# A graph network kernel: node rows split into a rounded part and a remainder, spread by float32r products

## The reference

```python
edge_index = jnp.stack([src, dst])
x = _layernorm(x + _L0_gnn_ref(...))   # relu projection, 2 x (messages of 8 edge types, sum by dst, GRU), out
x = _layernorm(x + _L1_gnn_ref(...))   # 3 x (relation matrices, mean per relation, sum by dst, root, relu)
x = _layernorm(x + _L2_gnn_ref(...))   # GCN: norm[:, None] * x[col], sum by row, W
x = _layernorm(x + _L3_gnn_ref(...))   # mean of edge attributes by row and by col, 2-layer MLP
...
            trans = jnp.einsum('nh,tdh->tnd', h, edge_W[l])
            msgs = trans[edge_type, src]
            agg = jax.ops.segment_sum(msgs, dst, num_segments=num_nodes)
            h = _gru_cell(agg, h, gru_wih[l], gru_whh[l], gru_bih[l], gru_bhh[l])
```

## Time and profile before

| what | value |
|---|---|
| median of 3 runs | 2964.3 us (2952.74 to 2971.47) |
| span of the profiled execution | 2969.2 us |
| PE matmul busy | 2492.2 us, 84% |
| PE weight loads busy | 2211.7 us, 74% |
| DVE busy | 1808.3 us, 61% |
| POOL busy | 1585.9 us, 53% |
| ACT busy | 868.5 us, 29% |
| HBM traffic | 174 GB/s over the span |

### The profile page before, as it was taken

One profiled execution on the slowest core, in us unless ns is written; L12 is line 12 of the kernel. 1 busy time (PEld: TensorE's weight loads), 2 busy tenths in 40 slices (PEclk: granted clock), 3 DMA queues, 4 the chain that ended last, 5 costly groups with the idle time before them and its releaser, 6 DMA issues.

```text
span 2969.2 us, 45704 instructions
## 1 busy us (share of the span) xinstructions
PE 2492.2 (84%) x15625; PEld 2211.7 (74%) x15625; DVE 1808.3 (61%) x6126; ACT 868.5 (29%) x1546; POOL 1585.9 (53%) x1706
## 2 busy tenths in 40 slices
PE   7587878888687899746999998998989897878798
PEld 3366666666387889436999997888988886777797
DVE  4565656575576777423876655676865554433585
ACT  2355555554354111213222231111311110443102
POOL 0656666663577666542566626666456665565200
PEclk9789888888799999857999999999999999898899
DMA  7312112110398666106888887877788774565793
GB/s 273 111 50 53 51 51 53 51 52 25 103 281 260 166 173 170 38 27 210 274 272 270 269 266 231 240 228 211 238 273 251 226 234 134 174 213 198 232 267 105
DMA packets 271515, 520.11 MB, mean 175 GB/s; under 512 B 61999, under 2 KB 115554, under 8 KB 270501
## 3 DMA queue, kind: packets, MB, share of 16 engines
q1 hardware_dynamic: 185053, 289.49, 31.2%
q0 software_dynamic: 86224, 227.59, 26.6%
HBM read 323.93 MB, written 192.99 MB: 174 GB/s over the span
## 4 chain that ended last, share of the span: by engine, by line
PE 69%; issue 10%; DMA 7%; DVE 6%; another core or an unknown queue 4%; ACT 2%; POOL 2%; SPq 0%; DVEq 0%; POOLq 0%; ACTq 0%
PE ps L1058 21%; PE ps L1030 10%; PE ps L892 7%; PE ps L1043 6%; PE ps L1245 5%; PE ps L1289 4%; PE ps L886 4%; PE ps L878 4%; DMA chunks<-xs 2%; DMA rec<-chunks,idx 2%; DMA srow<-lanes_of_slots 1%; DVE shot L2033 1%; POOL attributes L744 1%; PE ps L1112 1%
## 5 line engine op out<-in xcount | busy, mean ns | idle before, releaser
L735 POOL DMA_INDIRECT rec<-chunks,idx x596 | 588.5, 987 | 500.5 <-PE ps L1058 184.9
L1058 PE MATMUL ps<-dhot,rec 128*128 128x168 f32 x4768 | 757.2, 312 | 70.4 <-issue 35.3
L1058 PEld LDWEIGHTS ps<-dhot,rec 128*128 128x128 f32 x4768 | 703.8, 194 | 99.6 <-issue 77.6
L2054 DVE TENSOR_SCALAR dhot<-iota,dcode 128x168 f32<-128x168 f32 x2384 | 584.6, 311 | 216.7 <-remote 102.4
L1030 PE MATMUL ps<-hrow,shot 126*128 126x128 f32 x4000 | 516.3, 284 | 63.8 <-issue 29.5
L735 POOL DMA_INDIRECT msg<-messages,idx_buf x416 | 398.2, 957 | 307.3 <-issue 189.7
L1030 PEld LDWEIGHTS ps<-hrow,shot 126*128 126x128 f32 x4000 | 493.7, 199 | 81.7 <-issue 65.9
L1386 ACT ACTIVATE xs<-ps 128x512 f32<-128x512 f32 x500 | 295.1, 597 | 763.5 <-PE ps L1030 393.8
L744 POOL DMA_INDIRECT attributes<-w,rank_to x352 | 353.2, 1004 | 213.1 <-issue 102.2
L2033 DVE TENSOR_SCALAR shot<-srow,lane_no 126x512 f32<-126x512 uint8 x500 | 230.2, 486 | 117.4 <-PE ps L1030 51.2
L892 PE MATMUL ps<-big,lane1h 128*128 128x300 f32 x832 | 231.6, 432 | 9.3 <-issue 8.0
(11 more groups left out here) (304 smaller groups left out, 2538.6 us busy)
## 6 DMA issues: line engine op xcount, KB each, us to landing
chunks<-xs SPq DMA_DIRECT2D x375, 256.0 KB
tmp<-inverse_counts SPq DMA_DIRECT2D x36, 1008.0 KB
chunks<-xs SPq DMA_DIRECT2D x125, 258.0 KB
srow<-lanes_of_slots SPq DMA_DIRECT2D x100, 320.0 KB
grec<-chunks SPq DMA_DIRECT2D x125, 256.0 KB
messages<-big SPq DMA_DIRECT2D x25, 504.0 KB
trow<-lanes_of_targets SPq DMA_DIRECT2D x30, 320.0 KB
rec<-chunks,idx POOLq DMA_INDIRECT x596
```

Of the source, the lines that this page charges most:

```text
L735: eng.indirect_dma_start(buf, None, table, bass.IndirectOffsetOnAxis(ap=index, axis=0)).then_inc(sem, 16)
L1058: last = mm(ps[:, 4 + i % 2, (v % 3) * WT:(v % 3 + 1) * WT], rec[:, v % RS, j * P:(j + 1) * P], dhot[:, v % DS, j * WT:(j + 1) * WT], star ...
L2054: last = vec.tensor_scalar(dhot[:, v % DS, j * WT:(j + 1) * WT], iota[:, 0:WT], dcode[:, v, j:j + 1], None, ALU.is_equal)
```

## The change

`shot`, `thot`, `hrow` and `yrows` become float32r. ACT's copy from PSUM so leaves a rounded row in `hrow`. DVE then subtracts it from what is still in PSUM and keeps the remainder, also float32r (`keep_lows`, for the GCN `keep_target_lows` into `ylows`). In `spread_slots` and `spread_target` each float32 product becomes two float32r products into the same PSUM columns, one with the rounded rows and one with the remainders. PE's waits for `rows_kept` and `gcn_rows` become waits for `lows_kept`.

The remainders need room. For layer 1 they lie over `x`, which SP loads again from its input after layer 1's tiles; for layers 2 to 4 they lie over `nodes`, which SP stores to HBM in layer 1 and loads back after layer 4's tiles. The lists `code`, `idx`, `dcode` and `deg_part` move to the buffers of the layers, and several semaphores are merged into `window_step` and `degree`. The path for graphs that don't fit the slots (`general`, not taken here) adds both parts of `yrows` again.

```diff
+F32R = mybir.dt.float32r
...
+        nodes_d = nc.dram_tensor("node_counts", (P, NP), F32).ap()
...
-        x = sb("x", [P, NV])
+        with nc.sbuf_tensor("x", [P, NV], F32) as x:
+            pass
+        low_1 = sb("low_1", [P, TB, P], F32R)
         h = sb("h", [P, NV])
         res = sb("res", [P, NV])
         acc = sb("acc", [P, NP])
-        nodes = sb("nodes", [P, NP])
+        with nc.sbuf_tensor("nodes", [P, NP], F32) as nodes:
+            pass
+        low_2 = sb("low_2", [P, NB, P], F32R)
         tmp = sb("tmp", [P, 8, 512])
...
-                hrow = two("hrow", [P, TB, P])
...
+                hrow = two("hrow", [P, TB, P], F32R)
                 srow = two("srow", [P, NS, QS * SPAN], U8)
-                shot = two("shot", [P, SS, SPAN])
+                shot = two("shot", [P, SS, SPAN], F32R)
...
-                yrows = three("yrows", [P, NYB, P])
+                yrows = three("yrows", [P, NYB, P], F32R)
+                ylows = three("ylows", [P, NYB, P], F32R)
                 trow = three("trow", [P, NS, YW * SPAN], U8)
-                thot = three("thot", [P, SS, SPAN])
+                thot = three("thot", [P, SS, SPAN], F32R)
...
+        def lows(k):
+
+            return low_1 if k == 1 else low_2
+
...
+                    eng.dma_start(nodes_d, nodes[:]).then_inc(q("nodes_moved"), 16)
+                    after(eng, "stage1_mm", 1, NQ)
+                    eng.dma_start(x[:], xT_d).then_inc(q("loaded_x"), 16)
...
+                after(eng, "stage1_mm", 4, NQ)
+                eng.dma_start(nodes[:], nodes_d).then_inc(q("nodes_moved"), 16)
...
             def turn_rows(k, c):
 
                 if k >= 3 and c >= 1:
-                    after(eng, "rows_kept", k, c)
+                    after(eng, "lows_kept", k, c)
                 elif k < 3 and c >= 2:
-                    after(eng, "rows_kept", k, c - 1)
+                    after(eng, "lows_kept", k, c - 1)
                 for b in blocks_of(c):
                     j = b - c * CB
                     last = mm(ps[0:BS, ROW_BANKS[k][c % 2], j * P:(j + 1) * P], block_of(feed(k), b), wt("ident"),
...
-                    after(eng, "rows_kept", k, sb_ // CB + 1)
+                    after(eng, "lows_kept", k, sb_ // CB + 1)
...
-                    last = mm(ps[:, STAGE1_BANKS[i % 3], j * P:(j + 1) * P], shot[0:BS, i % SS, j * P:(j + 1) * P],
-                              hrow[0:BS, sb_, :], start=True, stop=True)
+                    out, lanes = ps[:, STAGE1_BANKS[i % 3], j * P:(j + 1) * P], shot[0:BS, i % SS, j * P:(j + 1) * P]
+                    mm(out, lanes, hrow[0:BS, sb_, :], start=True, stop=False)
+                    last = mm(out, lanes, lows(k)[0:BS, sb_, :], start=False, stop=True)
...
             def target_rows(u):
                 eng.wait_ge(q("x_scaled"), unit_chunk(u) + 1)
                 if u >= 2:
-                    eng.wait_ge(q("gcn_rows"), u - 1)
+                    after(eng, "lows_kept", GCN, u - 1)
...
+                eng.wait_ge(q("nodes_moved"), 32)
...
-                    last = mm(ps[:, STAGE1_BANKS[v % 3], j * P:(j + 1) * P], thot[0:nodes_of(c), v % SS, j * P:(j + 1) * P],
-                              yrows[0:nodes_of(c), c, :], start=True, stop=True)
+                    out, lanes = ps[:, STAGE1_BANKS[v % 3], j * P:(j + 1) * P], thot[0:nodes_of(c), v % SS, j * P:(j + 1) * P]
+                    mm(out, lanes, yrows[0:nodes_of(c), c, :], start=True, stop=False)
+                    last = mm(out, lanes, ylows[0:nodes_of(c), c, :], start=False, stop=True)
                 last.then_inc(q("stage1_mm"), 1)
...
+                    elif kind == "turn":
+                        keep_lows(j, n)
...
+            def keep_lows(k, c):
+                after(eng, "rows_kept", k, c + 1)
+                n = len(blocks_of(c))
+                rows_ = hrow[0:BS, c * CB:c * CB + n, :].rearrange("p a b -> p (a b)").bitcast(F32)
+                vec.tensor_tensor(lows(k)[0:BS, c * CB:c * CB + n, :].rearrange("p a b -> p (a b)"),
+                                  ps[0:BS, ROW_BANKS[k][c % 2], 0:n * P], rows_, ALU.subtract).then_inc(q("lows_kept"), 1)
...
+            def keep_target_lows(u):
+                n, m = len(y_unit(u)), nodes_of(y_unit(u)[-1])
+                eng.wait_ge(q("gcn_rows"), u + 1)
...
+                else:
+                    vec.tensor_tensor(ylows[0:BS, u * CB:u * CB + n, :].rearrange("p a b -> p (a b)"),
+                                      ps[0:BS, 6 + u % 2, 0:n * P],
+                                      yrows[0:BS, u * CB:u * CB + n, :].rearrange("p a b -> p (a b)").bitcast(F32),
...
-            for i in range(NCH):
+            for i in range(NCH + 2):
                 gru(0, i)
-                if i == 2:
+                if i >= 2:
+                    keep_lows(1, i - 2)
+                if i == 3:
                     place_cells()
...
+                    if c == 0:
+                        eng.wait_ge(q("loaded_x"), 4 * 16)
...
-            for c in range(NCH):
-                ln_apply(0, c)
+            eng.wait_ge(q("nodes_moved"), 16)
+            for c in range(NCH + 2):
+                if c < NCH:
+                    ln_apply(0, c)
+                if c >= 2:
+                    keep_lows(2, c - 2)
...
-                elif kind == "unit" and n == 0:
-                    vec.memset(xo[:, :, 4 * P:], 0.0)
-                    for v in range(THOT_AHEAD):
-                        target_hot(v)
-                    st.do(vec.tensor_scalar(gcn_lo[:], src1[:], ok_f[:], 1.0, ALU.mult, ALU.subtract))
+                elif kind == "unit":
+                    if n == 0:
+                        vec.memset(xo[:, :, 4 * P:], 0.0)
+                        for v in range(THOT_AHEAD):
+                            target_hot(v)
+                        st.do(vec.tensor_scalar(gcn_lo[:], src1[:], ok_f[:], 1.0, ALU.mult, ALU.subtract))
+                    keep_target_lows(n)
```

More of the change, by code:

```diff
@@ L143 @@
     "ln_spread": NCH, "ln_out": NCH,
-    "rows_mm": NCH, "rows_kept": NCH, "shot": NQ, "stage1_mm": NQ, "x1_evac": NQ, "win_mm": NW, "dhot": NW,
+    "rows_mm": NCH, "rows_kept": NCH, "lows_kept": NCH, "shot": NQ, "stage1_mm": NQ, "x1_evac": NQ, "win_mm": NW, "dhot": NW,
     "agg_evac": NTRI, "xf_mm": NGRP, "acc_evac": NGRP,
 }
-FIRST_RUN = {n: 1 for n in ("rows_mm", "rows_kept", "shot", "stage1_mm", "x1_evac", "win_mm", "dhot", "agg_evac", "xf_mm",
+FIRST_RUN = {n: 1 for n in ("rows_mm", "rows_kept", "lows_kept", "shot", "stage1_mm", "x1_evac", "win_mm", "dhot", "agg_evac", "xf_mm",
                             "acc_evac")}
@@ L269, in two @@
                     return layer_buffers.enter_context(nc.sbuf_tensor(name, shape, dt))
-                hrow = two("hrow", [P, TB, P])
+                idx = two("idx", [P, NWP], I32)
+                code = two("code", [P, NTILE])
+                dcode = two("dcode", [P, NWP, 4])
+                deg_part = two("deg_part", [P, NQ])
+                hrow = two("hrow", [P, TB, P], F32R)
                 srow = two("srow", [P, NS, QS * SPAN], U8)
-                shot = two("shot", [P, SS, SPAN])
+                shot = two("shot", [P, SS, SPAN], F32R)
                 xs = two("xs", [P, XS, RECORD_COLS])
@@ L1136, in _ @@
                     table(0, "edge0_0", h, i - 1)
-            eng.wait_ge(q("diag_ready"), 1)
-            mm(ps[:, 7, 0:2 * NG], wb("ones", NG, P), base_diag[:], start=True, stop=True).then_inc(q("base_mm"), 1)
-            eng.wait_ge(q("far_lanes"), 1)
-            mm(ps[:, 7, 0:1], wt("ones"), flags[:, 0:1], start=True, stop=True).then_inc(q("far_lanes_mm"), 1)
+            eng.wait_ge(q("window_step"), 1)
+            mm(ps[:, 7, 0:2 * NG], wb("ones", NG, P), base_diag[:], start=True, stop=True).then_inc(q("window_step"), 1)
+            eng.wait_ge(q("window_step"), 3)
+            mm(ps[:, 7, 0:1], wt("ones"), flags[:, 0:1], start=True, stop=True).then_inc(q("window_step"), 1)
             eng.wait_ge(q("loaded_rest"), 16)
@@ L1165, in _ @@
                 if i == 3:
-                    after(eng, "rows_kept", 1, 2)
+                    after(eng, "lows_kept", 1, 2)
                     eng.wait_ge(q("cells_known"), 1)
@@ L1201, in spread_dinv @@
             def spread_dinv(c):
-                eng.wait_ge(q("degree_inv"), 1)
+                eng.wait_ge(q("degree"), 3)
                 if c >= 1:
@@ L1228, in dst_means @@
                     eng.wait_ge(q("dst_inv"), 1)
-                    eng.wait_ge(q("gcn_rows"), YU)
+                    after(eng, "lows_kept", GCN, YU)
                 if c >= 2:
@@ L1239, in spread_target @@
                 if v % YW == 0 and c % CB == 0:
-                    eng.wait_ge(q("gcn_rows"), c // CB + 1)
+                    after(eng, "lows_kept", GCN, c // CB + 1)
                 if v >= 3:
@@ L1519, in _ @@
             eng.wait_ge(q("degree"), 1)
-            act(deg[0:BS, 1, :], deg[0:BS, 0, :], ACT.Sqrt).then_inc(q("deg_sqrt"), 1)
```

(7 more changed lines are left out.)

29 lines of the change are left out of this document (17 added, 12 removed).

## The result

The kernel after takes 3178.97 us (median, 3173.47 to 3188.69) against 2959.51 for the kernel before beside it: ratio 1.0732, 95% interval 1.0687 to 1.0777. It is slower by 219 us. The forecast of 2886 and its range are both missed, on the side of rival 1, and beyond it. The profiled execution spans 3171.6 us against 2969.2.

The account below looks back on a forecast made before the run. PE was taken to bound layers 2 to 4, DMA layer 1's tiles, nothing alone the GCN tiles. -79 - 3 - 20 + 14 + 3 + 3 + 4 = -78 us gave 2891 profiled, 2886 median; range 2780 to 3010.

Parts of the forecast that it names:

- rival 1: Tile products: one half of the float32r record keeps its rate, 110 ns; 2989 us (2970 to 3010), chance 0.27.
- I take 56: Tile products: the lowest price, 56 ns per float32r record, with streaming and weight load both at single rate.
- the 102 us: Gain expected from the shorter record: 79 us in layers 2 to 4, 3 in layer 1's tiles, 20 in GCN tiles.
- the -78 us of the forecast: Whole kernel: the net change after gains in three tile stages and the added parts, giving 2891 us profiled.
- the middle one: Tile products: the second of three prices, 110 ns: one record per product, one half at today's rate.
- 14 us to the turns: Layers 3 and 4: remainders delay DVE's queue, 1.5 us for each of 14 turns, 21 us, counted as 14.
- 24 to all added parts: Added costs: turns 14 us, layer starts 3, remainders among the GRU's steps 3, GCN units 4.
- one stall of 1.5 us a turn: Layers 3 and 4: PE's loss behind each of 14 turns, 1.5 us (1 to 2.2).
- 79 + 3 + 20: Gains in us at 56 ns: layers 2 to 4, layer 1's tiles and GCN tiles, in that order.
- The cap that I set: Layers 2 to 4: gain per stretch limited to DMA's room under share 0.92; 105 us, three quarters taken, 79.
- Rival 3: Layers 2 to 4: DMA or DVE takes over more, win 50 us, 2945; chance within the forecast's 0.54.
- my case: Whole kernel: the forecast at 56 ns per record, 2886 us, own range 2760 to 2945, chance 0.54.

## Why the prediction was wrong

**The steps that failed** are three: the price ("I take 56"), the clock (the sum has no term for it), and the 102 us that the price was to bring. Between the -78 us of the forecast and the +219 measured lie 297. The products account for 251 of them (-102 in the sum, +149 measured alone), the remainders for 34 (24 and 58), and 12 are left.

**The price.** The bounds were drawn rightly: the price is the middle one, 110 ns, by the earlier trace rows, where one-column products already showed loads of 4-byte weights that come no closer than 100 ns. I chose 56 by an argument about what the change is for, one-pass products, and not by a row. It holds for the stream (226 ns at 512 columns) and not for the rest of the record. The row that I had for the load, the shorter load record of the transposes, 141 ns instead of 192, excluded nothing: a record's duration is not the distance. The float32r load lasts 192 and its distance is 111; the transposes' load lasts 141 and their distance was 110 as well.

**What no case held.** Rival 1 priced the record rightly and gave 2989; the kernel takes 3179. Its missing term is the clock, at which the prediction put nothing and for which it gave no reason. By the clock at each start, 190 of the 4000 records at L1030 ran at 0.50 before; in the kernel after they are 1565 of 4000, and 1117 of 1192 in the GCN (191 before). 1000 of them make layer 1's tiles: 1000 x 213 ns = 213 of 224 us. In the GCN 1117 x 213 + 75 x 111 = 246 of 298. The other 565 lie in layers 2 to 4, 448 more than before; at 102 ns each these cost 46 us of PE, of which the stage shows about 20 (the products alone, with 317 more: 8 + 4 + 8). Take 70 and 63 off the span of 3171.6 and 3039 is left; with those 20 off too, 3019. That is an estimate of the kernel at rival 1's terms, near the 3010 of its upper end; what it has above 2989 is mostly the remainders, below.

**The remainders.** The mechanism was right: DVE's queue behind ACT, 1.90 us of idle PE where 1 to 2.2 were expected. The size was off. I gave 14 us to the turns and 24 to all added parts; alone they cost 58, the close turns of layers 3 and 4 28 of it (14 each, above). I counted one stall of 1.5 us a turn. The last rounds of a layer lose more, 5.8 us apart instead of 2.5; and between the first two turns there are 13.1 us instead of 5.4 (15.3 instead of 5.8 in layer 4), because ACT's copy itself came late and a window and its `transform` stood behind the `dhot` that DVE could not yet make:
```profile
1674.26 0.60 ACT L1394 ACTIVATE hrow<-ps 126x512 f32<-126x512 f32 x1 [2.31 <-remote]
...
1674.89 0.69 DVE L2130 TENSOR_TENSOR low<-ps,hrow 126x512 f32<-126x512 f32 x1 [7.54 <-ACT hrow L1394]
...
1676.50 2.61 PE L1075 MATMUL ps<-dhot,rec 128*128 128x168 f32 x8 [5.03 <-DVE dhot L2076]
```
These are rows of the timeline of the remainders-alone kernel behind its turn at 1670.88: DVE sits idle for 7.54 us and PE for 5.03. Where the other 30 of the 58 lie I can't say from the one profiled execution of it, whose span is only 36 us above that of before (it is the shortest of its executions, and that of before the longest).

**The value of a shorter record.** Even the 56 ns would not have paid as I summed it. Terms of 79 + 3 + 20 = 102 us stood for it; at 56 ns and without remainders (the bfloat16 products) 12 were measured. Layers 2 to 4 gave 7 (1105.1 to 1098.0), not 79; the other chip may hide some of the gain, but the whole kernel, compared on one chip, gives no more than 27 (the lower end of the ratio, 0.9909). The cap that I set was DMA's share against a ceiling of 0.92. Behind 1700 us the share stayed at 0.82 and less, so there bandwidth is not what stopped the gain. By the waits it is the order of things: PE waits for gathers, which run only six buffers ahead, for ACT's evacuation, and as issue. And where PE idled more, its clock was lower. Rival 3 named this and gave it too little.

**What held.** One record per product. The copies of `x` and `nodes` cost nothing to be seen (layer 1's sums 240.4 and 241.8 us, the end unchanged). PE waits for `shot` by 1 to 2 us after a turn. The mark "I am wrong if the distance is above 100" was the one met. Two other signs went against my case as well: in layers 2 to 4 PE's busy share was 0.91 (1097 of 1205 us) and not 0.85, and DMA's fell to 0.75.

## What to carry to other kernels

Price a product by the distance of records from start to start, never by a duration, and by the slower of stream and weight load. With 128 columns and 4-byte weights the distance was 111 ns and stayed there at 64 columns; the stream was seen to set it only at 512. At 128 columns two float32r products cost what one float32 product does (2 x 111 and 2 x 112 ns), so the split wins nothing. Before taking work off TensorE, ask what its clock will do: a stage made of float32r products between waits ran at 1.2 GHz with the engine full, and a float32 product mixed in made it faster. An operation that waits for another engine goes into an in-order queue behind all that others are about to need: moving the remainders by two places was worth 24 us, in the kernel with bfloat16 parts.

## What the hardware showed that I had not expected

- float32r products with 128 columns: 111 ns from start to start at the full clock, 213 at the low one; 111 with 64 columns, 119 with 256, 226 with 512. bfloat16 with 128 columns: 56 and 107 (the second in the tiles of the kernel with bfloat16 products alone).
- 800 float32r products after a rest, PE busy for each of 170 us: clock 0.50 throughout. Float32 after the same rest: 1.00 after 19 records. Why float32r does not raise the clock, these runs don't tell; nor was it tried to give a stage of the kernel some float32 products ahead of its tiles, though the GCN's tiles had the full clock for 10 us behind 16 of them.
- Entered at 1.00, 600 float32r records of 128 columns kept it, 34 of 64 columns did not.
